# Embeddings stored feature by feature in blocks of 32 samples, Gram products over samples 16 apart

## The chip, the cores and the metric

The kernel runs on one core of one Trainium2 chip. Times are device microseconds of one launch; the kernel's time is the median of its runs.

## The reference, cut to what matters

A recommendation tower for 2,048 samples. Each of 27 tables gives a sample one row of 128 numbers. All pairs of these 27 rows are multiplied (351 dot products a sample), 16 dense inputs are appended, and three layers follow.

```python
e = jnp.stack([tbl_0[ids[:, 0]], ..., tbl_26[ids[:, 26]]], axis=1)   # (2048, 27, 128)
interactions = jnp.einsum('bnd,bmd->bnm', e, e)
z = interactions[:, i, j]                    # i < j, 351 columns
h = jnp.concatenate([z, dense_ctx], axis=1)  # 367 columns
h = jnp.maximum(h @ W_top1 + b_top1, 0.0)    # 512
h = jnp.maximum(h @ W_top2 + b_top2, 0.0)    # 256
y = h @ W_top3                               # 1
```

Eleven tables have 1,000 rows, the other 16 have 1,250 to 125,000. All data are float32.

## The kernel before, in words

The batch is worked in 8 pairs of tiles, 128 samples a tile, 256 a pair. The index p is the pair, t the tile in it.

**Embeddings.** For 16 features GpSimd gathers the rows from HBM by indirect DMA (L543), one sample a partition. TensorE transposes them, four features into one PSUM bank (L583), and ScalarE copies the bank into `emb` (`take_turned`, L871). The 11 small tables lie in SBUF, each split in a rounded part and a rest. VectorE makes one-hot matrices from the ids (L747), TensorE multiplies both parts with them (L572, L574), and ScalarE copies the result into `emb` (`take_lookup`, L852). Most lookups serve two pairs at once; the half for the next pair goes to `held` (L851) and from there to `emb` at the start of the next pair (`place_held`, L862). `emb` holds on each of 128 partitions (one for each of the 128 numbers of a row) tile, sample and feature, the feature innermost, so that the 27 features of a sample are neighbours.

**Gram products.** `gram_products` (L586 to L603) takes four samples a step. Two matmuls, one for each half of the array's output rows, have two samples' 54 columns each as stationary and as moving operand. Their result has the products of each sample with itself on its diagonal blocks, and the products between the two samples beside them, which nobody uses. Eight such steps fill a PSUM bank, four banks make a tile. A plain float32 matmul is two records in the trace, so there are 2,048 records for 1,024 matmuls. ScalarE copies each bank into `gram` (`take_gram`, L882), its columns turned so that the samples of a pair lie innermost.

**The way to layer 1.** The two samples of a half are apart in `gram`'s partitions. SyncE stores the four quarters of `gram` to HBM (`store_products`, L371 to L377, 32 partitions each, for which `stored_rows`, L307, gives the rows) and loads them back as `z` (`load_z`, L415), with every product on a partition of its own. The reload order folds the symmetric matrix. ScalarE puts the dense inputs into `z` (`place_dense`, L904), in the order of the quarters; SyncE had loaded them to one of two buffers (`load_dense`, L360). Layer 1 is L617 on TensorE with L891 on ScalarE, which also sets the samples' order for layer 2, L626; VectorE does the last one (L784, L789). The last pair is worked tile by tile at the end (L644, L655, L897).

**Order of the work.** Every engine has its order written out. Each engine's program goes pair by pair. TensorE in pair p does the lookups of p with transposes between them, layer 1 of p - 1 with the second tile's transposes, Gram products of tile 0, layer 2 of p - 1, Gram products of tile 1. ScalarE follows it bank by bank. Three PSUM banks take transposes and lookups, two take Gram products. In pair 0 the tables also have to be loaded, rounded (L813), shown in PSUM (L824) and split (L768, VectorE). `picks`, an 11 x 11 identity, is the weight with which TensorE spreads the first ids (L671, L677); it has a buffer of its own.

Of the kernel before, what the change touches and what calls it, by code (L numbers as in the profile page):

```python
# [32 lines left out]
F32R = mybir.dt.float32r  # L33
# [95 lines left out]
GROUPS = P // QUARTERS  # L129
GRAM_COLS = ABREAST * NF  # L130
HALF_ROWS = P // HALVES
GRAM_PART = HALF_ROWS + GRAM_COLS
GROUPS_A_BANK = 8
GRAM_BANKS = 2
# [52 lines left out]
def build(nc, dense_t, ids_rows, ids_onehot, gathered_tables, onehot_tables, w1, w2, w3, b1, b2, out):  # L187
    with ExitStack() as ctx:
# [11 lines left out]
        rows = sb("rows", [P, TILES, NG, DIM])  # L200
        emb = sb("emb", [P, TILES, P, NF])
        gram = sb("gram", [P, ABREAST, NF, RUN])
# [13 lines left out]
        b2_row, w3_row = rows23[:, 0, :], rows23[:, 1, :]  # L216
        dense = sb("dense", [P, 2, PAIR])
        held = sb("held", [P, HELD, PAIR])
        h1 = sb("h1", [P, M1, PAIR])

        y = sb("y", [P, 2, TILES])
        last_row = dense[0:1, 0, 0:P]

# [15 lines left out]
        first_ids = table_lo[0:NO, NO - 1, 0:2 * PAIR // DIM, :].rearrange("k j d -> k (j d)")  # L239
        picks = sb("picks", [NO, NO], F32R)  # L240

# [13 lines left out]
        HALF_TABLE = part // GRAM_BANKS  # L255

        idx_loaded = [sem(f"idx_loaded{i}") for i in range(2)]
        ids_first = sem("ids_first")
# [5 lines left out]
        weights_loaded = sem("weights_loaded")  # L264
        dense_loaded = [sem(f"dense_loaded{i}") for i in range(2)]
        dense_placed = sem("dense_placed")
# [40 lines left out]
        def stored_rows(q):  # L307

            half, s = divmod(q, ABREAST)
            row = half * HALF_ROWS + s * NF  # L310

            pad = PAD if q == QUARTERS - 1 else 0
            return row - pad, row - pad + STORE_ROWS, PAD - pad

# [17 lines left out]
        def store_position(engine, t, q):  # L332
            row, end, to = stored_rows(q)
            engine.dma_start(last_products[t, to:to + STORE_ROWS, :, q, :],
                             gram[row:end, q % ABREAST, :, t * GROUPS:(t + 1) * GROUPS]
                             ).then_inc(last_products_out[t], 16)
# [4 lines left out]
        def _(sp):  # L341
# [14 lines left out]
            def load_dense(p):  # L356
                if p >= 2:

                    sp.wait_ge(dense_placed, p - 1)
                sp.dma_start(dense[DENSE_AT:DENSE_AT + DENSE, p % 2, :], dense_t[:, p * PAIR:(p + 1) * PAIR]  # L360
                             ).then_inc(dense_loaded[p % 2], 16)

# [8 lines left out]
            def store_products(p):  # L371

                sp.wait_ge(gram_taken, (p + 1) * PAIR_GRAMS)
                for q in range(QUARTERS):
                    row, end, to = stored_rows(q)
                    sp.dma_start(products[p % 2, to:to + STORE_ROWS, :, q, :], gram[row:end, q % ABREAST, :, :]  # L376
                                 ).then_inc(products_out, 16)  # L377
# [68 lines left out]
            load_dense(0)  # L446
            load_dense(1)
            for i in lookups_of(1)[:IDS_SLOTS]:
                load_ids(i)

            for p in range(PAIRS):
                if p > 0:
                    for i in lookups_of(p)[IDS_SLOTS:]:
                        load_ids(i)
                    store_products(p - 1)
                    load_z(p - 1)
                    if p + 1 < PAIRS:
                        load_dense(p + 1)
                if 0 < p < LAST:
                    for i in lookups_of(p + 1)[:IDS_SLOTS]:  # L460
                        load_ids(i)
                if 0 < p < PAIRS - 1:
                    store_y(p - 1)
# [85 lines left out]
        def _(pe):  # L549
# [36 lines left out]
            def gram_products(p, t):  # L586

                pe.wait_ge(emb_taken, tile_end(p, t))
                for i in range(TILE_GRAMS):
                    a = p * PAIR_GRAMS + t * TILE_GRAMS + i  # L590
                    if a >= GRAM_BANKS:

                        pe.wait_ge(gram_taken, a - GRAM_BANKS + 1)
                    ps = gram_ps[a % GRAM_BANKS]
                    for b in range(GROUPS_A_BANK):
                        group = i * GROUPS_A_BANK + b
                        for half in range(HALVES):
                            first = group * QUARTERS + half * ABREAST
                            samples = emb[:, t, first:first + ABREAST, :].rearrange("d s f -> d (s f)")
                            last = nc.tensor.matmul(  # L600
                                ps[half * HALF_ROWS:half * HALF_ROWS + GRAM_COLS, b * GRAM_COLS:(b + 1) * GRAM_COLS],
                                samples, samples, start=True, stop=True)
                    last.then_inc(gram_full, 1)  # L603
# [17 lines left out]
            def layer2(p):  # L621

                pe.wait_ge(mlp_taken, p * M1 + M1)
                for t in range(TILES):
                    for k in range(M1):
                        last = nc.tensor.matmul(mlp_ps[t][:, 0:HID2], h1[:, k, t * P:(t + 1) * P], w2_sb[:, k, :],  # L626
                                                start=k == 0, stop=k == M1 - 1)
                    last.then_inc(mlp_full, 1)
# [95 lines left out]
        def _(dve):  # L724
            def make_onehot(i, part):
# [19 lines left out]
                if i < NO:  # L745
# [3 lines left out]
                    *operands, ALU.is_equal).then_inc(onehot_ready, 1)  # L749

            dve.wait_ge(ids_first, 16)
            nc.vector.tensor_copy(first_ids, first_ids_i).then_inc(ids_first_f, 1)
# [56 lines left out]
        def _(act):  # L809
# [35 lines left out]
            def take_lookup(i):  # L845
# [4 lines left out]
                if pairs == 2:  # L850
                    nc.scalar.copy(held[:, k if k < len(SETS[0]) else k - len(SETS[0]), :], ps[:, PAIR:2 * PAIR]).then_inc(held_taken, 1)  # L851
                nc.scalar.copy(emb[:, :, :, NG + k], ps[:, 0:PAIR].rearrange("d (t b) -> d t b", t=TILES)  # L852
                               ).then_inc(emb_taken, 1)

            def place_held(p):

                for n, (group, p0, pairs) in enumerate(LOOKUPS):
                    if p0 == p - 1 and pairs == 2:

                        act.wait_ge(held_taken, sum((pairs - 1) * len(SETS[g]) for g, _, pairs in LOOKUPS[:n + 1]))  # L860
                        slot, size = NG + SETS[group][0], len(SETS[group])
                        nc.scalar.copy(emb[:, :, :, slot:slot + size].rearrange("d t b f -> d (t b) f"),  # L862
                                       held[:, 0:size, :].rearrange("d f b -> d b f")).then_inc(held_placed, 1)

                        act.wait_ge(held_placed, sum(pairs - 1 for _, _, pairs in LOOKUPS[:n + 1]))

            def take_turned(p, t, n):
                act.wait_ge(turned, turns_before(p, t, n + 1))
                first, size = turn_bank(n)
                ps = emb_ps[BANK_INDEX[("turn", p * TILES + t, n)] % EMB_BANKS]  # L870
                nc.scalar.copy(emb[:, t, :, first:first + size],  # L871
                               ps[:, 0:size * P].rearrange("d (f b) -> d b f", f=size)).then_inc(emb_taken, 1)

            def take_gram(p, t):
# [3 lines left out]
                for i in range(TILE_GRAMS):  # L878
# [3 lines left out]
                    nc.scalar.copy(  # L882
                        gram[0:GRAM_PART, :, :, g0:g0 + GROUPS_A_BANK].rearrange("r s j g -> r (s j) g"),
                        gram_ps[a % GRAM_BANKS][0:GRAM_PART, 0:GROUPS_A_BANK * GRAM_COLS].rearrange(
                            "r (g c) -> r c g", c=GRAM_COLS)).then_inc(gram_taken, 1)

            def take_layer1(chunk, m):
                act.wait_ge(mlp_full, chunk + m + 1)
                samples = mlp_ps[m % 2][:, 0:PAIR].rearrange("p (r t g) -> p t g r", r=QUARTERS // TILES, t=TILES)
                placed = h1[:, m, :].rearrange("p (t g r) -> p t g r", t=TILES, r=QUARTERS // TILES)  # L890
                nc.scalar.activation(placed, samples, ACT.Relu, bias=b1_sb[:, m:m + 1]).then_inc(mlp_taken, 1)  # L891

            def take_last_layer1(t, m):
                act.wait_ge(mlp_full, LAST * MLP_CHUNKS + t * LAST_CHUNKS + m + 1)
                samples = last1_ps[m][:, 0:P].rearrange("p (q g) -> p g q", q=QUARTERS)
                placed = h1[:, m, t * P:(t + 1) * P].rearrange("p (g q) -> p g q", q=QUARTERS)
                nc.scalar.activation(placed, samples, ACT.Relu, bias=b1_sb[:, m:m + 1]).then_inc(mlp_taken, 1)  # L897

            def place_dense(p):

                act.wait_ge(dense_loaded[p % 2], (p // 2 + 1) * 16)
# [8 lines left out]
            nc.scalar.copy(picks[:, :], ident[0:NO, 0:NO]).then_inc(picks_placed, 1)  # L910
            ahead = EMB_BANKS + 1
# [98 lines left out]
```

## Time and profile before

| | |
|---|---|
| median of 3 runs | 347.89 us (347.8 to 348.27) |
| span of the profiled execution | 346.3 us |
| TensorE matmuls busy | 331.1 us |
| TensorE weight loads busy | 282.8 us |
| VectorE busy | 219.4 us |
| ScalarE busy | 184.7 us |
| GpSimd busy | 242.9 us |
| 16 DMA engines | 44.06 MB moved |

The span is from the first to the last instruction of one profiled execution; the time of a run also holds what lies around it, here 1.6 us to the median. PE is TensorE's matmuls, PEld its weight loads, which run beside them. ACT is ScalarE, DVE VectorE, POOL GpSimd, SP SyncE; a q behind a name is the engine's sequencer, which issues DMAs. Matmuls are pipelined: the mean duration of one is longer than the time between two starts, so the pace of a row of matmuls is read from the time of the whole row.

### The profile page before, as it was taken

Reading aid. Unit: us, or ns where it says so; the run is one execution under the profiler, and the core shown is the slowest. Engines: PE = TensorE matmul, PEld = TensorE weight load, DVE = VectorE, ACT = ScalarE, POOL = GpSimd, SP = SyncE. Lnnn points to the kernel's source line nnn. Section 1 sums busy time; section 2 is a strip of 40 time slices with the busy share of each in tenths; the row PEclk is TensorE's granted clock in tenths of the full one; section 3 lists DMA queues with packets and bytes.
Section 4 is the critical chain, followed back from the end, with each engine's and each line's share of the span. In section 5 each row is a group of like instructions: output and inputs, shape, how many; then the busy total and the mean of one; then the engine's idle time right before and its main releaser. Section 6 shows DMA issues by size and latency. Waiting matters only on the chain.

```text
span 346.3 us, 8212 instructions
## 1 busy us (share of the span) xinstructions
PE 331.1 (96%) x3478; PEld 282.8 (82%) x3478; DVE 219.4 (63%) x160; ACT 184.7 (53%) x315; POOL 242.9 (70%) x263
## 2 busy tenths in 40 slices
PE   2899999999999999999999999999999999998995
PEld 1667878887898888887898889887888889997894
DVE  5899997599427971499626991399724990360021
ACT  4898975533646354633646355633447346554521
POOL 6777777777777777777777777777777777777200
PEclk9999999999999999999999999999999999999999
DMA  6975795655237772768229772677327552572440
GB/s 169 222 178 168 225 252 142 156 157 135 67 55 157 146 158 55 107 173 178 83 55 157 146 160 55 89 197 177 83 57 134 131 112 57 85 168 72 85 81 8
DMA packets 53981, 44.06 MB, mean 127 GB/s; under 512 B 39810, under 2 KB 43983, under 8 KB 53945
## 3 DMA queue, kind: packets, MB, share of 16 engines
q1 hardware_dynamic: 43993, 26.52, 35.1%
q0 software_dynamic: 8192, 16.79, 21.3%
q8 instruction: 28, 0.46, 0.6%
q10 hardware_dynamic: 1760, 0.22, 0.4%
q14 instruction: 8, 0.07, 0.1%
HBM read 36.43 MB, written 7.09 MB: 126 GB/s over the span
## 4 chain that ended last, share of the span: by engine, by line
PE 86%; DMA 6%; SPq 3%; ACT 2%; issue 1%; DVE 1%; DVEq 0%
PE emb_ps L572 21%; PE emb_ps L574 20%; PE gram_ps L600 16%; PE mlp_ps L617 11%; PE mlp_ps L626 7%; PE emb_ps L583 7%; DMA h<-tbl_rows 3%; DMA products<-gram 1%; DMA gram<-tbl_rows 1%; PE emb_ps L644 1%; SPq L376 1%; DMA z<-products 1%; SPq L369 1%; PE mlp_ps L671 1%; PE mlp_ps L655 1%
## 5 line engine op out<-in xcount | busy, mean ns | idle before, releaser
L543 POOL DMA_INDIRECT rows<-tbl_rows,idx x256 | 242.0, 945 | 78.9 <-issue 74.4
L747 DVE TENSOR_TENSOR onehot<-ids_b,row_id 125x2048 fp32r<-125x2048 int32 x72 | 158.9, 2279 | 33.3 <-PE emb_ps L574 33.3
L572 PE MATMUL emb_ps<-onehot,table_hi 125*128 125x512 f32 (+1 forms) x400 | 147.6, 378 | 5.6 <-DVE table_lo L768 4.0
L574 PE MATMUL emb_ps<-onehot,table_lo 125*128 125x512 f32 (+1 forms) x400 | 143.0, 367 | 0.0
L572 PEld LDWEIGHTS emb_ps<-onehot,table_hi 125*128 125x128 f32 x400 | 76.0, 190 | 21.5 <-DVE table_lo L768 4.8
L574 PEld LDWEIGHTS emb_ps<-onehot,table_lo 125*128 125x128 f32 x400 | 76.1, 190 | 10.7
L600 PEld LDWEIGHTS gram_ps<-emb 128*54 128x54 f32 x2048 | 53.6, 130 | 5.6 <-issue 3.5
L600 PE MATMUL gram_ps<-emb 128*54 128x54 f32 x2048 | 55.8, 214 | 1.7 <-ACT emb L852 0.8
L851 ACT COPY held<-emb_ps 128x256 f32<-128x256 f32 x38 | 14.1, 371 | 75.9 <-PE emb_ps L574 75.8
L784 DVE TENSOR_TENSOR mlp_ps<-mlp_ps,rows 128x256 f32<-128x256 f32 x14 | 6.1, 433 | 76.5 <-PE mlp_ps L626 76.5
L882 ACT COPY gram<-gram_ps 118x432 f32<-118x432 f32 x64 | 33.2, 519 | 39.5 <-PE gram_ps L600 39.2
L871 ACT COPY emb<-emb_ps 128x512 f32<-128x512 f32 x64 | 45.5, 710 | 0.0
L617 PE MATMUL mlp_ps<-z,w_sb 126*128 126x256 f32 x168 | 41.2, 380 | 1.0 <-DMA z<-products 1.0
L583 PE MATMUL emb_ps<-ident,rows 128*128 128x128 f32 x256 | 38.8, 274 | 0.0
L852 ACT COPY emb<-emb_ps 128x256 f32<-128x256 f32 x50 | 34.4, 688 | 7.9 <-PE emb_ps L574 7.9
L583 PEld LDWEIGHTS emb_ps<-ident,rows 128*128 128x128 f32 x256 | 31.0, 140 | 7.2 <-issue 0.5
L747 DVE TENSOR_TENSOR onehot<-z,mlp_ps 125x2048 fp32r<-125x2048 int32 (+1 forms) x16 | 33.5, 2114 | 2.0 <-PE mlp_ps L671 1.3
L617 PEld LDWEIGHTS mlp_ps<-z,w_sb 126*128 126x128 f32 x168 | 30.1, 190 | 4.7 <-DMA z<-products 1.2
L626 PE MATMUL mlp_ps<-w_sb,h 128*128 128x256 f32 x112 | 26.0, 386 | 0.0
L626 PEld LDWEIGHTS mlp_ps<-w_sb,h 128*128 128x128 f32 x112 | 20.7, 190 | 2.9
L891 ACT ACTIVATE h<-mlp_ps,columns 128x256 f32<-128x256 f32 x28 | 13.3, 474 | 17.6 <-PE mlp_ps L617 17.6
L862 ACT COPY emb<-held 128x1280 f32<-128x1280 f32 (+1 forms) x7 | 19.2, 2741 | 0.2
(49 smaller groups left out, 102.6 us busy)
## 6 DMA issues: line engine op xcount, KB each, us to landing
ids_b<-ids_onehot SPq DMA_DIRECT2D x33, 256.0 KB, 5.5
products<-gram SPq DMA_DIRECT2D x28, 216.0 KB
gram<-tbl_rows SPq DMA_DIRECT2D x9, 480.0 KB
rows<-tbl_rows,idx POOLq DMA_INDIRECT x256, 2.9
z<-products SPq DMA_DIRECT2D x14, 126.0 KB
h<-tbl_rows SPq DMA_DIRECT2D x2, 480.0 KB
z<-products SPq DMA_DIRECT2D x7, 112.0 KB
w_sb<-w SPq DMA_DIRECT2D x1, 768.0 KB, 5.8
```

The source lines that it names most:

```text
L543: pool.indirect_dma_start(out=rows[:, t, f, :], out_offset=None, in_=gathered_tables[f], in_offset=bass.IndirectOffsetOnAxis(ap=idx[:, p, ...
L572: nc.tensor.matmul(ps[:, 0:width], table_hi[0:ROWS, k, j, :], columns[:, c, :], start=j == 0, stop=False)
L574: last = nc.tensor.matmul(ps[:, 0:width], table_lo[0:ROWS, k, j, :], columns[:, c, :], start=False, stop=j == ROWS_PER - 1)
L583: last = nc.tensor.transpose(ps[:, f * P:(f + 1) * P], rows[:, t, first + f, :], ident[:])
L600: last = nc.tensor.matmul(ps[half * HALF_ROWS:half * HALF_ROWS + GRAM_COLS, b * GRAM_COLS:(b + 1) * GRAM_COLS], samples, samples, start=Tr ...
L617: last = nc.tensor.matmul(ps[:, 0:PAIR], w1_sb[0:k, s, m * P:(m + 1) * P], z[0:k, s, :], start=s == 0, stop=s == STEPS - 1)
L626: last = nc.tensor.matmul(mlp_ps[t][:, 0:HID2], h1[:, k, t * P:(t + 1) * P], w2_sb[:, k, :], start=k == 0, stop=k == M1 - 1)
L747: nc.vector.tensor_tensor(onehot[0:ROWS, seq % ONEHOT_RING, 0:own * width].rearrange("p (j b) -> p j b", b=width), *operands, ALU.is_equal ...
L852: nc.scalar.copy(emb[:, :, :, NG + k], ps[:, 0:PAIR].rearrange("d (t b) -> d t b", t=TILES)).then_inc(emb_taken, 1)
L862: nc.scalar.copy(emb[:, :, :, slot:slot + size].rearrange("d t b f -> d (t b) f"), held[:, 0:size, :].rearrange("d f b -> d b f")).then_in ...
L871: nc.scalar.copy(emb[:, t, :, first:first + size], ps[:, 0:size * P].rearrange("d (f b) -> d b f", f=size)).then_inc(emb_taken, 1)
L882: nc.scalar.copy(gram[0:GRAM_PART, :, :, g0:g0 + GROUPS_A_BANK].rearrange("r s j g -> r (s j) g"), gram_ps[a % GRAM_BANKS][0:GRAM_PART, 0: ...
```

## The change

`emb` becomes `[partition, tile, quadrant of 32 samples, 28 slots, 32 samples]`: the samples of a feature are neighbours, in runs of 32. Slot 28 holds zeros, cleared once by VectorE, and TensorE waits for that once. A Gram product takes two samples 16 apart, so the columns (feature, sample) are 56 elements with one step of 16 elements between them. They come out with the two samples alternating, so a quarter's rows in `gram` are every second partition. One PSUM bank now serves one quadrant. All copies into `emb`, `place_dense` and the layer 1 copies follow the new order, and layer 2 takes every second column of `h1` as weights. To make room, the dense inputs have one buffer (a load waits until the previous pair's were placed), and `picks` lies in an unused corner of the last table.

```diff
-GRAM_COLS = ABREAST * NF
+QUADRANTS = 4
+QUADRANT = P // QUADRANTS
+APART = QUADRANT // ABREAST
+SLOTS = NF + 1
+GRAM_COLS = ABREAST * SLOTS
-GROUPS_A_BANK = 8
+GROUPS_A_BANK = APART // HALVES
...
-        emb = sb("emb", [P, TILES, P, NF])
+        emb = sb("emb", [P, TILES, QUADRANTS, SLOTS, QUADRANT])
-        dense = sb("dense", [P, 2, PAIR])
+        dense = sb("dense", [P, PAIR])
-        picks = sb("picks", [NO, NO], F32R)
+        picks = table_lo[0:NO, NO - 1, 2 * PAIR // DIM, 0:NO]
...
         def stored_rows(q):
-            half, s = divmod(q, ABREAST)
-            row = half * HALF_ROWS + s * NF
-            pad = PAD if q == QUARTERS - 1 else 0
-            return row - pad, row - pad + STORE_ROWS, PAD - pad
+            s, half = divmod(q, HALVES)
+            pad = PAD if half == HALVES - 1 else 0
+            row = half * HALF_ROWS + s - pad * ABREAST
+            return slice(row, row + (STORE_ROWS - 1) * ABREAST + 1, ABREAST), s, PAD - pad
...
             def load_dense(p):
-                if p >= 2:
-                    sp.wait_ge(dense_placed, p - 1)
-                sp.dma_start(dense[DENSE_AT:DENSE_AT + DENSE, p % 2, :], dense_t[:, p * PAIR:(p + 1) * PAIR]
-                             ).then_inc(dense_loaded[p % 2], 16)
+                if p >= 1:
+                    sp.wait_ge(dense_placed, p)
+                sp.dma_start(dense[DENSE_AT:DENSE_AT + DENSE, :], dense_t[:, p * PAIR:(p + 1) * PAIR]
+                             ).then_inc(dense_loaded, 16)
...
             load_dense(0)
-            load_dense(1)
...
                     load_z(p - 1)
-                    if p + 1 < PAIRS:
-                        load_dense(p + 1)
+                    load_dense(p)
...
             def gram_products(p, t):
+                if p == 0 and t == 0:
+                    pe.wait_ge(pads_cleared, 1)
...
-                        group = i * GROUPS_A_BANK + b
                         for half in range(HALVES):
-                            first = group * QUARTERS + half * ABREAST
-                            samples = emb[:, t, first:first + ABREAST, :].rearrange("d s f -> d (s f)")
+                            samples = emb[:, t, i, :, :].rearrange(
+                                "d k (s j) -> d (k s) j", s=ABREAST)[:, :, half * GROUPS_A_BANK + b]
...
-                        last = nc.tensor.matmul(mlp_ps[t][:, 0:HID2], h1[:, k, t * P:(t + 1) * P], w2_sb[:, k, :],
+                        last = nc.tensor.matmul(mlp_ps[t][:, 0:HID2], h1[:, k, t:PAIR:TILES], w2_sb[:, k, :],
...
+            nc.vector.memset(emb[:, :, :, NF, :], 0.0).then_inc(pads_cleared, 1)
             dve.wait_ge(ids_first, 16)
...
-                nc.scalar.copy(emb[:, :, :, NG + k], ps[:, 0:PAIR].rearrange("d (t b) -> d t b", t=TILES)
-                               ).then_inc(emb_taken, 1)
+                nc.scalar.copy(emb[:, :, :, NG + k, :], ps[:, 0:PAIR].rearrange(
+                    "d (t q j) -> d t q j", t=TILES, q=QUADRANTS)).then_inc(emb_taken, 1)
...
-                        nc.scalar.copy(emb[:, :, :, slot:slot + size].rearrange("d t b f -> d (t b) f"),
-                                       held[:, 0:size, :].rearrange("d f b -> d b f")).then_inc(held_placed, 1)
+                        nc.scalar.copy(emb[:, :, :, slot:slot + size, :].rearrange("d t q f j -> d (t q) f j"),
+                                       held[:, 0:size, :].rearrange("d f (q j) -> d q f j", j=QUADRANT)
+                                       ).then_inc(held_placed, 1)
...
-                nc.scalar.copy(emb[:, t, :, first:first + size],
-                               ps[:, 0:size * P].rearrange("d (f b) -> d b f", f=size)).then_inc(emb_taken, 1)
+                nc.scalar.copy(emb[:, t, :, first:first + size, :],
+                               ps[:, 0:size * P].rearrange("d (f q j) -> d q f j", f=size, q=QUADRANTS)
+                               ).then_inc(emb_taken, 1)
...
-                        gram[0:GRAM_PART, :, :, g0:g0 + GROUPS_A_BANK].rearrange("r s j g -> r (s j) g"),
+                        gram[0:GRAM_PART, :, :, g0:g0 + GROUPS_A_BANK],
                         gram_ps[a % GRAM_BANKS][0:GRAM_PART, 0:GROUPS_A_BANK * GRAM_COLS].rearrange(
-                            "r (g c) -> r c g", c=GRAM_COLS)).then_inc(gram_taken, 1)
+                            "r (g c s) -> r s c g", s=ABREAST, c=SLOTS)[:, :, 0:NF, :]).then_inc(gram_taken, 1)
...
-                samples = mlp_ps[m % 2][:, 0:PAIR].rearrange("p (r t g) -> p t g r", r=QUARTERS // TILES, t=TILES)
-                placed = h1[:, m, :].rearrange("p (t g r) -> p t g r", t=TILES, r=QUARTERS // TILES)
+                samples = mlp_ps[m % 2][:, 0:PAIR].rearrange("p (q x g) -> p x q g", q=QUARTERS, g=GROUPS_A_BANK)
+                placed = h1[:, m, :].rearrange("p (x q g) -> p x q g", q=QUARTERS, g=GROUPS_A_BANK)
...
-                        z[DENSE_PART:DENSE_PART + DENSE, STEPS - 1, c0:c1].rearrange("d (q g) -> d q g", q=QUARTERS),
-                        dense[DENSE_AT:DENSE_AT + DENSE, p % 2, c0:c1].rearrange("d (g q) -> d q g", q=QUARTERS))
+                        z[DENSE_PART:DENSE_PART + DENSE, STEPS - 1, c0:c1].rearrange(
+                            "d (q x g) -> d q x g", q=QUARTERS, g=GROUPS_A_BANK),
+                        dense[DENSE_AT:DENSE_AT + DENSE, c0:c1].rearrange(
+                            "d (x q g) -> d q x g", q=QUARTERS, g=GROUPS_A_BANK))
```

## Rows read from the trace of the kernel before

**Rows 1.** The page: busy time and share of each engine; granted clock in slices.
```profile
PE 331.1 (96%) x3478; PEld 282.8 (82%) x3478; DVE 219.4 (63%) x160; ACT 184.7 (53%) x315; POOL 242.9 (70%) x263
...
PEclk9999999999999999999999999999999999999999
```

**Rows 2.** The page: the chain that ended last, by engine and line.
```profile
PE emb_ps L572 21%; PE emb_ps L574 20%; PE gram_ps L600 16%; PE mlp_ps L617 11%; PE mlp_ps L626 7%; PE emb_ps L583 7%; DMA h<-tbl_rows 3%; DMA products<-gram 1%; DMA gram<-tbl_rows 1%; PE emb_ps L644 1%; SPq L376 1%; DMA z<-products 1%; SPq L369 1%; PE mlp_ps L671 1%; PE mlp_ps L655 1%
```

**Rows 3.** Waits on TensorE's queues: who waited <- for whom: us, times, longest.
```profile
PE mlp_ps L617 <- DMA z<-products: 1.0, 1, 1.0
PE gram_ps L600 <- ACT emb L852: 0.8, 1, 0.8
PE gram_ps L600 <- ACT emb L871: 0.7, 1, 0.7
PE emb_ps L572 <- ACT emb L852: 0.7, 2, 0.4
...
PEld emb_ps L572 <- ACT emb L852: 2.0, 4, 0.6
```

**Rows 4.** ScalarE's groups by form: xcount | busy us, mean ns | idle before.
```profile
L871 ACT COPY emb<-emb_ps 128x512 f32<-128x512 f32 x64 | 45.5, 710 | 0.0
L852 ACT COPY emb<-emb_ps 128x256 f32<-128x256 f32 x50 | 34.4, 688 | 7.9 <-PE emb_ps L574 7.9
L882 ACT COPY gram<-gram_ps 118x432 f32<-118x432 f32 x64 | 33.2, 519 | 39.5 <-PE gram_ps L600 39.2 <-issue 0.3
L851 ACT COPY held<-emb_ps 128x256 f32<-128x256 f32 x38 | 14.1, 371 | 75.9 <-PE emb_ps L574 75.8
L862 ACT COPY emb<-held 128x1280 f32<-128x1280 f32 x4 | 10.1, 2532 | 0.1
L862 ACT COPY emb<-held 128x1536 f32<-128x1536 f32 x3 | 9.1, 3019 | 0.1
L904 ACT COPY z<-dense 16x256 f32<-16x256 f32 x7 | 4.5, 646 | 0.2
L904 ACT COPY z<-dense 16x128 f32<-16x128 f32 x2 | 0.7, 418 | 1.4 <-issue 1.4
L930 ACT COPY rows<-mlp_ps 128x512 f32<-128x512 f32 x1 | 0.6, 586 | 0.2 <-PE mlp_ps L664 0.2
```

**Rows 5.** The chain in order of time, first pair: start us, us, what.
```profile
44.36 0.55 ACT emb L852
...
54.00 0.67 ACT emb L852
```

**Rows 6.** Busy time in a stretch (PE, PEld, DVE, ACT, POOL); VectorE's last-but-one split.
```profile
40.00:50.00 10.00, 8.95 (x64) 7.54 (x63) 10.00 (x10) 8.55 (x15) 7.56 (x9) 1.00 1.05 287
...
47.06 1.27 DVE L768 TENSOR_TENSOR table_lo<-gram,gram_ps 125x512 fp32r<-125x512 f32 x2
```

**Rows 7.** The chain in order of time, around the last pair.
```profile
304.08 4.54 DMA products<-gram
...
324.98 0.66 ACT emb L871
```

**Rows 8.** The chain in order of time: a lookup, transposes, layer 1, a Gram tile.
```profile
26.82 0.23 PE emb_ps L574
...
91.19 0.44 PE emb_ps L583 x4
91.62 1.30 PE mlp_ps L617 x6
...
93.36 3.42 PE gram_ps L600 x128
```

**Rows 9.** The weight loads of L600: duration ns min/median/max, first and last start.
```profile
L600 PEld LDWEIGHTS gram_ps<-emb x2048: 124/130/130, 54.7 to 328.9; 128*54 128x54 f32 x187
```

**Rows 10.** SyncE in order of time, pair 1: the issue of the dense load.
```profile
72.35 0.53 SPq L360 DMA_DIRECT2D dense<-dense_t  x1
```

**Rows 11.** All engines at the start, in order of time.
```profile
2.88 0.41 DVE L752 CAST table_lo<-rows 11x512 fp32r<-11x512 int32 x1 [2.88 <-DMA rows<-ids_onehot]
```

More of the change, by code:

```diff
@@ L221, in build @@
         y = sb("y", [P, 2, TILES])
-        last_row = dense[0:1, 0, 0:P]
+        last_row = dense[0:1, 0:P]
         row_id_i = z[:, STEPS - 1, 0:ROWS_PER].bitcast(I32)
@@ L255, in build @@
         HALF_TABLE = part // GRAM_BANKS
+        pads_cleared = sem("pads_cleared")
         idx_loaded = [sem(f"idx_loaded{i}") for i in range(2)]
@@ L264, in build @@
         weights_loaded = sem("weights_loaded")
-        dense_loaded = [sem(f"dense_loaded{i}") for i in range(2)]
+        dense_loaded = sem("dense_loaded")
         dense_placed = sem("dense_placed")
@@ L332, in store_position @@
         def store_position(engine, t, q):
-            row, end, to = stored_rows(q)
+            rows_of, s, to = stored_rows(q)
             engine.dma_start(last_products[t, to:to + STORE_ROWS, :, q, :],
-                             gram[row:end, q % ABREAST, :, t * GROUPS:(t + 1) * GROUPS]
+                             gram[rows_of, s, :, t * GROUPS:(t + 1) * GROUPS]
                              ).then_inc(last_products_out[t], 16)
@@ L374, in store_products @@
                 for q in range(QUARTERS):
-                    row, end, to = stored_rows(q)
-                    sp.dma_start(products[p % 2, to:to + STORE_ROWS, :, q, :], gram[row:end, q % ABREAST, :, :]
+                    rows_of, s, to = stored_rows(q)
+                    sp.dma_start(products[p % 2, to:to + STORE_ROWS, :, q, :], gram[rows_of, s, :, :]
                                  ).then_inc(products_out, 16)
@@ L894, in take_last_layer1 @@
                 act.wait_ge(mlp_full, LAST * MLP_CHUNKS + t * LAST_CHUNKS + m + 1)
-                samples = last1_ps[m][:, 0:P].rearrange("p (q g) -> p g q", q=QUARTERS)
-                placed = h1[:, m, t * P:(t + 1) * P].rearrange("p (g q) -> p g q", q=QUARTERS)
+                samples = last1_ps[m][:, 0:P].rearrange("p (q x g) -> p x q g", q=QUARTERS, g=GROUPS_A_BANK)
+                placed = h1[:, m, t * P:(t + 1) * P].rearrange("p (x q g) -> p x q g", q=QUARTERS, g=GROUPS_A_BANK)
                 nc.scalar.activation(placed, samples, ACT.Relu, bias=b1_sb[:, m:m + 1]).then_inc(mlp_taken, 1)
             def place_dense(p):
-                act.wait_ge(dense_loaded[p % 2], (p // 2 + 1) * 16)
+                act.wait_ge(dense_loaded, (p + 1) * 16)
                 spans = [(0, PAIR)] if p < LAST else [(t * P, (t + 1) * P) for t in range(TILES)]
@@ L904, in place_dense @@
                     last = nc.scalar.copy(
-                        z[DENSE_PART:DENSE_PART + DENSE, STEPS - 1, c0:c1].rearrange("d (q g) -> d q g", q=QUARTERS),
-                        dense[DENSE_AT:DENSE_AT + DENSE, p % 2, c0:c1].rearrange("d (g q) -> d q g", q=QUARTERS))
+                        z[DENSE_PART:DENSE_PART + DENSE, STEPS - 1, c0:c1].rearrange(
+                            "d (q x g) -> d q x g", q=QUARTERS, g=GROUPS_A_BANK),
+                        dense[DENSE_AT:DENSE_AT + DENSE, c0:c1].rearrange(
+                            "d (x q g) -> d q x g", q=QUARTERS, g=GROUPS_A_BANK))
                 last.then_inc(dense_placed, 1)
             act.wait_ge(ident_steps, 3)
-            nc.scalar.copy(picks[:, :], ident[0:NO, 0:NO]).then_inc(picks_placed, 1)
+            nc.scalar.copy(picks, ident[0:NO, 0:NO]).then_inc(picks_placed, 1)
             ahead = EMB_BANKS + 1
```

## The prediction
> **What bounds the kernel now.** I read the page's busy line first [rows 1]: TensorE is busy 331.1 of 346.3 us, ScalarE 184.7, VectorE 219.4. Then the chain that ended last [rows 2]: TensorE carries 86% of it, and the Gram products (L600) are 16%, 55 us. Last the waits of TensorE's own queues [rows 3], which tell what a faster ScalarE could give back: TensorE's matmuls waited for ScalarE's embedding copies (L852, L871) 0.8 + 0.7 + 0.7 us, and its weight loads up to 2.0 us in one row, at mostly the same moments. So the kernel is bound by TensorE; ScalarE is a side road. The change makes ScalarE's work lighter and touches what TensorE reads. These two ends decide it. The clock plays no part: the page has it granted in full all through [rows 1].
>
> The sum is made against the profiled span, 346.3 us. The median of the runs, 347.89, lies 1.6 us above it; I carry that over unchanged. A measurement of this kernel can tell a change of about 0.2%, 0.7 us, from none.
>
> **ScalarE's copies.** Two rows give its price for data that lie in a row: 371 ns for 256 elements (L851) and 586 for 512 (L930), so 0.84 ns an element and 156 ns to begin [rows 4]. The copies whose elements jump pay more: L852 (256 elements, each 27 from the next) 688 ns, L862 2532 ns for 1280 and 3019 for 1536, L871 (runs of four) 710 ns for 512. After the change all of them write and read runs of 32 or more. By the two prices they take 371, 1231, 1446 and 586 ns. That frees 50 x 0.317 + 4 x 1.30 + 3 x 1.57 + 64 x 0.124 = 33.7 us of ScalarE. L882 keeps 432 elements and runs of eight; at 519 ns it already stands at the price of a row (156 + 432 x 0.84 = 519), so its jumps in PSUM cost nothing and it stays.
>
> Nearly all of that lies beside TensorE's work. What lies on the path:
> - At 54.00 the last lookup of the first pair is copied (0.67 us) while TensorE stands before its first Gram product [rows 5]. The copy gets 0.3 us shorter: **-0.3 us**.
> - At 44.36 a copy of L852 holds up a lookup by 0.4 us [rows 3, 5]. But VectorE is busy 10.00 of the 10.00 us from 40 to 50 [rows 6], and the lookup after the next one needs its table split, which ends only at 48.33. TensorE would only come early to that: 0, at most -0.3 us.
> - At 324.98 the last turned bank (L871, 0.66 us) holds the last Gram tile [rows 7]: **-0.1 us**.
> These are all the long ones in the list [rows 3]; past the first pair, the last is the only one. Sum of the copies: **-0.4 us**, between -1.0 (0.3 more at 44.36 and 0.3 more at the last tile) and 0.
>
> **The Gram products, number of columns.** 54 columns become 56, in the stationary and the moving operand. A tile's 128 records (64 pairs, one record of a pair for each half of the array) take 3.42 us, 53.4 ns a pair [rows 8]. The wide matmuls give the pace of plain float32: 0.44 us for four of 128 columns, 1.30 for six of 256, so 107 ns for 128 more columns, 0.84 ns each. At that pace 54 columns stream in 45 ns and 56 in 47: both are shorter than the 53.4 ns between pairs, so something fixed may set the interval. If the columns set it, two more cost 2 x 0.84 = 1.7 ns, times 1,024 pairs (2,048 records [rows 9]) 1.7 us. Bounds 0 and +1.7; I take **0**, since the stream is 6 ns shorter than the interval even with 56.
> The Trainium skill (TensorE: Matmul & The Clock Gate, Back-to-back issue gap) has matmuls of 1 to 64 columns all cost about 60 cycles. By that this term is 0 too, against +1.7 by columns; the 26.7 ns a record here speaks for the page.
>
> **The Gram products, where they read.** The two samples' features lay as 54 neighbours. Now each column is 16 elements, 64 bytes, from the last, for both operands. No TensorE row here reads so, so I bound it. From below 0: a plain float32 column takes 0.84 ns, while the lookups read theirs at 0.23 us for 512, 0.45 ns each [rows 8], so the read path can do twice what a Gram record asks, and a reader that fell to half of that would still keep up. From above: ScalarE's copy of the dense inputs (L904) reads SBUF with a step of four elements, 646 ns for 256 and 418 for 128, so 1.78 ns an element against 0.84 [rows 4]. TensorE at 1.78 would need 100 ns for 56 columns, some 105 a pair, and lose 52 x 1,024 = 53 us. The two ends are far apart. I take **0**: the nearest row is one of TensorE itself, and it shows the reserve; but that row reads neighbours, and here two halves and two loads read at once, so the doubt is large and is the main rival.
>
> **Layer 2** takes its weights (L626) with a step of two. A load runs beside the matmul before it; were its stream of 128 columns (107 ns at 0.84 each) doubled, 214 would still fit the 217 of a matmul of 256 [rows 8]. 0, at most 112 records x 15 ns = 1.7 us.
>
> **Stores and loads.** The four stores of a pair keep their bytes and runs; their rows are now every second partition. Only the last pair shows TensorE waiting for their result, 1.0 us [rows 3], behind a flight of the stores of 4.54 us [rows 7]. It stands there once, so everywhere else z lands ahead. I take 0, between -1.0 (that wait gone) and +2 (each store of the last pair half a microsecond slower).
> **Dense inputs in one buffer.** One 16 KB load leaves the start; the others move one pair later. Its new wait on SyncE is for the placement of the pair before. ScalarE makes that between the two Gram tiles of its pair, and SyncE comes to the load only after it has stored both tiles and issued the z loads, at 72.35 in pair 1 [rows 10]: no wait. Queued behind it are the id loads of the next pair and the store of y, as before. The data are due when that pair's first Gram tile is copied, which ends in pair 1 at 93.36 + 3.42 [rows 8], 24 us later; in the last pair they are placed after both Gram tiles. 0. Without that cover it would be one small load's landing, a few microseconds a pair.
> **Picks and pads.** Picks move into a corner of the last table, whose rewriting comes after their last use; no wait is added. Clearing the pads is one VectorE memset of 256 elements; its cast of 512 elements takes 0.41 us [rows 11], so less than that, within VectorE's 2.88 us of idleness at the start [rows 11], and TensorE asks for it at 54.7. 0; without that cover 0.4 us at most. The layer 1 copies and L904 get runs of eight; none is on the path.
>
> Sum: -0.4 + 0 + 0 = -0.4 us: **347.5 us**. This case's own range is 346.9 to 348.4.
>
> **Rivals.**
> 1. *TensorE pays for the jumps* (slower). Place: L600. It decides as soon as one column at a step of 64 bytes takes longer than 0.95 ns (53.4 over 56). For it: every SBUF access of ScalarE with a jump of 16 bytes or more costs it twice, L904, L852 and L862 alike. Against it: the reserve above. At 1.78 ns, 347.5 + 53 = 400.5 us; at just twice the stream, 94 + 3 ns a pair, 347.5 + 44 = 391.5. I put 396, the middle. Chance 0.35. Some 0.07 more for a shared reading port, where both halves queue for it: 190 ns a pair, +140 us, 488.
> The Trainium skill speaks for this rival: SBUF — State Buffer (Door 1: The DMA port swizzle) has lines of 16 bytes, and each access that crosses to a new line pays a penalty. It gives no size. ScalarE's rows agree; no row of TensorE here shows it.
> 2. *Columns set the interval.* 347.5 + 1.7 = 349.2. Chance 0.08.
> 3. *The lighter ScalarE gives back more* (faster): all waits on it go, and the last pair's z comes earlier: -1.0 and -0.6, 346.3. For it: the list of waits. Against: VectorE without a gap from 40 to 50 us. Chance 0.13.
> The change does what it says; only its worth is open.
>
> **How the numbers follow.** Forecast 0.37, rival 1 0.35 and 0.07, rival 2 0.08, rival 3 0.13. The range leaves out the shared port and a little of each side: 346.3 to 403. Faster by over 0.2% (under 347.2): rival 3 and 0.04 of the forecast, 0.17. Within: 0.32. Slower: rivals 1 and 2 and a trace of the forecast, 0.51. Signs are split, so the time is that of the likeliest single case.
>
> **What would show it.** Right: a Gram tile of 128 records still near 3.42 us; L852 near 371 ns, L871 near 586, L862 near 1231 and 1446; ScalarE busy near 151 us; the wait at the first Gram product shorter by 0.3. Wrong: a Gram tile of 6 us or more and a weight load of L600 well over 130 ns [rows 9] (rival 1); 3.53 us (rival 2); a longer z wait in the last pair.

## The result and the profile after

The changed kernel takes 393.38 us (median of 4 runs, 392.94 to 394.59) against 347.93 for the one before in the same job: a ratio of 1.1299, 95% interval 1.1275 to 1.1324. It is 45.5 us slower. The forecast was 347.5; the first rival, that TensorE pays for the jumps, had 391.5 to 400.5.

The page of the changed kernel, busy line and chain, against [rows 1, 2]:

```profile
PE 377.6 (96%) x3478; PEld 330.2 (84%) x3478; DVE 219.9 (56%) x161; ACT 155.3 (40%) x315; POOL 243.1 (62%) x263
...
PEclk9999999999999999999999999999999999999999
...
PE gram_ps L604 26%; PE emb_ps L575 20%; PE emb_ps L577 19%; PE mlp_ps L621 9%; PE emb_ps L586 7%; PE mlp_ps L630 7%; DMA h<-tbl_rows 3%; DMA products<-gram 1%; DMA z<-products 1%; PE emb_ps L648 1%; PE mlp_ps L675 1%; SPq L374 1%; SPq L381 1%; PE mlp_ps L659 0%; PE gram_ps L659 0%
```

ScalarE is busy 29.4 us less, VectorE and GpSimd the same, TensorE 46.5 us more, and its clock is granted as before. The Gram products (now L604) grew from 16% of the chain to 26%. The groups by form, against [rows 4, 9] (xcount | busy us, mean ns | idle before):

```profile
L604 PE MATMUL gram_ps<-emb 128*56 128x56 f32 x2048 | 102.7, 274 | 1.2 <-ACT emb L877 0.7 <-ACT emb L857 0.6
L604 PEld LDWEIGHTS gram_ps<-emb 128*56 128x56 f32 x2048 | 100.3, 190 | 4.8 <-issue 3.8 <-ACT emb L877 0.9
...
L877 ACT COPY emb<-emb_ps 128x512 f32<-128x512 f32 x64 | 38.0, 594 | 0.3
L889 ACT COPY gram<-gram_ps 120x432 f32<-120x432 f32 x64 | 33.2, 520 | 88.4 <-PE gram_ps L604 82.8 <-issue 5.6
...
L857 ACT COPY emb<-emb_ps 128x256 f32<-128x256 f32 x50 | 18.9, 378 | 10.7 <-PE emb_ps L577 10.7
...
L867 ACT COPY emb<-held 128x1280 f32<-128x1280 f32 x4 | 5.1, 1263 | 0.1
L867 ACT COPY emb<-held 128x1536 f32<-128x1536 f32 x3 | 4.4, 1477 | 0.1
```

ScalarE's copies fell nearly as read from its own rows: 378, 594, 1263 and 1477 ns where 371, 586, 1231 and 1446 were expected; L889, the old L882, stayed at 520. A weight load of a Gram product rose from 130 to 190 ns. The chain in order of time, against [rows 5, 7, 8] (start us, us, what):

```profile
54.72 12.62 PE gram_ps L604 x256
67.34 0.43 PE emb_ps L575
...
98.47 6.36 PE gram_ps L604 x109
...
233.00 6.37 PE gram_ps L604 x128
239.37 3.66 PE mlp_ps L630 x16
...
343.30 4.84 DMA products<-gram
...
368.12 0.56 ACT emb L877
```

The same places in the kernel before: its first two Gram tiles, which the next lookup ends, the second tile of a pair, and a row of layer 2. Behind them is the wait for z in the last pair, of the changed kernel ([rows 3] has it for the one before).

```profile
54.72 6.51 PE gram_ps L600 x234
...
62.22 0.43 PE emb_ps L572
...
96.78 3.65 PE mlp_ps L626 x16
100.43 3.37 PE gram_ps L600 x128
```
```profile
PE mlp_ps L621 <- DMA z<-products: 0.4, 1, 0.4
```

A Gram tile takes 6.36 or 6.37 us (the last of the last two pairs 6.39 and 6.44). Before, the first tile of a pair took 3.42 and the second 3.37. (A row of the trace can lack some records, x109 for instance; its time is that of the whole tile.) The first two tiles took 12.62 us; before they ended 7.50 us after their start (54.72 to 62.22), so 5.1 more now. The other 14 rows of the chain add up to 89.2 us against 47.65, 41.55 more. That makes 46.7 us. The wait for the last pair's z gave 0.6 back (1.0 to 0.4; why is not shown), the last turned bank 0.1, and the stretch from the last copy to the end of the trace was 0.5 shorter (2.3 against 2.8). What is left is 45.5, the difference of the spans (391.8 against 346.3). The other matmuls keep their pace, layer 2 with its weights at a step of two among them (3.66 against 3.65 us for 16 records). SyncE and TensorE show no wait for the dense buffer, the picks or the pads.

### The profile page after: what moved, and what is told of

Its sections match the earlier page's. It is cut to its first block, busy times and chain, and to the rows that moved or that the text cites. A ratio compares the mean times of both kernels' runs of the same rounds, so it can differ in the third digit from the quotient of the medians.

```text
span 391.8 us, 8214 instructions
## 1 busy us (share of the span) xinstructions
PE 377.6 (96%) x3478; PEld 330.2 (84%) x3478; DVE 219.9 (56%) x161; ACT 155.3 (40%) x315; POOL 243.1 (62%) x263
## 4 chain that ended last, share of the span: by engine, by line
PE 91%; DMA 5%; SPq 2%; issue 1%; ACT 1%; DVE 0%; DVEq 0%
PE gram_ps L604 26%; PE emb_ps L575 20%; PE emb_ps L577 19%; PE mlp_ps L621 9%; PE emb_ps L586 7%; PE mlp_ps L630 7%; DMA h<-tbl_rows 3%; DMA products<-gram 1%; DMA z<-products 1%; PE emb_ps L648 1%; PE mlp_ps L675 1%; SPq L374 1%; SPq L381 1%; PE mlp_ps L659 0%; PE gram_ps L659 0%
## 5 line engine op out<-in xcount | busy, mean ns | idle before, releaser
L604 PEld LDWEIGHTS gram_ps<-emb 128*56 128x56 f32 x2048 | 100.3, 190 | 4.8 <-issue 3.8
L604 PE MATMUL gram_ps<-emb 128*56 128x56 f32 x2048 | 102.7, 274 | 1.2 <-ACT emb L877 0.7
L889 ACT COPY gram<-gram_ps 120x432 f32<-120x432 f32 x64 | 33.2, 520 | 88.4 <-PE gram_ps L604 82.8
L877 ACT COPY emb<-emb_ps 128x512 f32<-128x512 f32 x64 | 38.0, 594 | 0.3
L857 ACT COPY emb<-emb_ps 128x256 f32<-128x256 f32 x50 | 18.9, 378 | 10.7 <-PE emb_ps L577 10.7
L829 ACT COPY gram_ps<-table_hi 125x512 f32<-125x512 f32 x22 | 12.3, 596 | 0.6 <-DVE table_lo L773 0.4
```

The source lines that it names most:

```text
L604: last = nc.tensor.matmul(ps[half * HALF_ROWS:half * HALF_ROWS + GRAM_COLS, b * GRAM_COLS:(b + 1) * GRAM_COLS], samples, samples, start=Tr ...
L857: nc.scalar.copy(emb[:, :, :, NG + k, :], ps[:, 0:PAIR].rearrange("d (t q j) -> d t q j", t=TILES, q=QUADRANTS)).then_inc(emb_taken, 1)
L877: nc.scalar.copy(emb[:, t, :, first:first + size, :], ps[:, 0:size * P].rearrange("d (f q j) -> d q f j", f=size, q=QUADRANTS)).then_inc(e ...
L889: nc.scalar.copy(gram[0:GRAM_PART, :, :, g0:g0 + GROUPS_A_BANK], gram_ps[a % GRAM_BANKS][0:GRAM_PART, 0:GROUPS_A_BANK * GRAM_COLS].rearran ...
```

## The experiments

Each is a single run with its profile unless a ratio is given. A time "against" another is against the kernel before in the same job. Where the text says wrong features or columns, the kernel multiplies other data than it should; the number of instructions is the same. "Tile" is a Gram tile's row in the chain, 128 records, or 64 pairs of records (one record of a pair for each half of the array). "Near" stands for 56 neighbouring columns, "line" for 16 bytes of SBUF that begin at a multiple of 16.

**e1: the change without its step.**
```diff
-                            samples = emb[:, t, i, :, :].rearrange(
-                                "d k (s j) -> d (k s) j", s=ABREAST)[:, :, half * GROUPS_A_BANK + b]
+                            flat = emb[:, t, i, :, :].rearrange("d k j -> d (k j)")
+                            c0 = (b * HALVES + half) * GRAM_COLS
+                            near = flat[:, c0:c0 + GRAM_COLS]
...
-                                samples, samples, start=True, stop=True)
+                                near, near, start=True, stop=True)
```


> The changed kernel, but both operands of a Gram product are 56 neighbours of the block (so it multiplies the wrong features); layout, copies, stores, 56 columns, dense buffer and picks are those of the change. Theory (only the 64-byte step costs): a Gram tile of 128 records takes 3.42 us, or 3.53 if columns set the interval; time 347.5 us, or 349.2. Rival (the stores of every second partition, the copies or the wider products carry part of the 45 us): well over 350 us, up to 393 if the step is innocent.

349.6 us against 348.6; ratio 1.0036, interval 1.0024 to 1.0048. Its row in the chain:
```profile
290.26 3.51 PE gram_ps L605 x128
```
All but 1 us is gone with the step. Layout, stores of every second partition, the single dense buffer and the picks are innocent of the 45 us. The tile is 3.51, not 3.42, although nothing but two columns was added to it.

**e9: the same with 54 columns** (`SLOTS = NF`, no clearing of pads).

> As e1 (neighbours for both operands, wrong features), with 27 slots and so 54 columns, and no clearing of pads: all of the change but the step and the two more columns. If two more columns cost 1.67 ns a pair: 50.0 ns a pair, tile 3.42 us, and 1.6 us less than e1, 0.1% under before or equal to it. If 28 slots cost nothing: the same as e1, 0.36% over before.

348.23 us against 348.55; ratio 0.9992, interval 0.9971 to 1.0012; its tile:
```profile
252.04 3.42 PE gram_ps L603 x128
```
Two columns more thus cost 0.09 us a tile, 1.4 us in 16 tiles: the columns do set the interval. What is left of the change, lighter copies included, cannot be told from no change.

**e2 and e3: one operand with the step.** As e1, but `samples, near` (weights apart) or `near, samples` (moving apart).

> Only the stationary operand has the 64-byte step, the moving one is 56 neighbours (wrong features). Theory A (each operand's reader pays by itself, and either sets the interval): Gram tile about 6.36 us, weight load about 190 ns, time 393. Theory B (the two share one budget of reads): tile about 4.9 us, time 370. Theory C (only the moving operand pays): tile 3.4 to 3.5, weight load 130 ns, time 348.

> Only the moving operand has the 64-byte step, the stationary one is 56 neighbours (wrong features). Theory A (each reader pays by itself): tile about 6.36 us, weight load back near 130 ns, time 393. Theory B (shared budget): 4.9 us, 370. Theory D (only weight loads pay): tile 3.4 to 3.5 us, time 348.

394.84 and 393.95 us, tiles of 6.42 and 6.38 us. Weight loads and matmuls of the two kernels, e2 first:
```profile
L607 PE MATMUL gram_ps<-emb 128*56 128x56 f32 x2048 | 103.6, 262 | 1.2 <-ACT emb L880 0.7 <-ACT emb L860 0.6
L607 PEld LDWEIGHTS gram_ps<-emb 128*56 128x56 f32 x2048 | 101.7, 191 | 4.8 <-issue 3.8 <-ACT emb L880 0.9
```
```profile
L607 PE MATMUL gram_ps<-emb 128*56 128x56 f32 x2048 | 102.9, 274 | 1.2 <-ACT emb L880 0.7 <-ACT emb L860 0.6
L607 PEld LDWEIGHTS gram_ps<-emb 128*56 128x56 f32 x2048 | 99.6, 146 | 4.8 <-issue 3.8 <-ACT emb L880 0.9
```
Either operand alone is enough for the whole price, and both together cost no more than one. So theory A holds, the one in which each operand pays by itself and the slower sets the interval. One detail of it missed: with neighbours again in e3, a weight load took 146 ns and not 130. The two runs also say what a repair needs: both operands must be free of the step.

**e4, e10, e5: other blocks, the right result.** The samples of a product are half a block apart, so blocks of 4 give a step of 8 bytes and blocks of 8 one of 16. e4 has 54 columns, e10 and e5 have 56.
```diff
-QUADRANTS = 4
+QUADRANTS = P // 4
...
-GROUPS_A_BANK = APART // HALVES
+GROUPS_A_BANK = 8
+GROUPS_A_BLOCK = APART // HALVES
```
(e5 has `P // 8` and, like e10, keeps the 28th slot; the Gram products pick block and place from b, and the layer 1 copies use `GROUPS_A_BLOCK`.)

> The same layout with blocks of 4 samples instead of 32 and 27 slots: the two samples of a product are 2 apart, so its 54 columns have a step of 2 elements, 8 bytes, and two of them share 16 bytes. The result is the reference's. Theory (what costs is a new 16-byte line for every column; two columns a line are enough for plain float32): tile 3.42 us, L852's copies about as fast as L871's before (runs of four), time 347.3 to 347.7, equal to before. Rival (any step costs): tile up to 6.4 us, 391.

> Blocks of 4 as in e4, but with the 28th slot, 56 columns at a step of 2. The result is the reference's. If the uneven 49 to 54 ns a pair of e4 (51.6 on average with 54 columns) come of blocks of 27 slots that end off a multiple of 32 bytes, the pairs are even here at 51.7 ns. Otherwise they are uneven again, about 53 ns, tile 3.6.

> Blocks of 8 samples, 56 columns with a step of 4 elements, 16 bytes: every column begins a new 16 bytes, though only a quarter of the change's step. The result is the reference's. Line theory (what counts is how many different 16-byte lines the columns touch, 1.67 ns a line): 96.7 ns a pair, tile 6.4 us, 393. Rival (the cost grows with the length of the step): tile between 3.5 and 5 us, 350 to 370.

e4: 349.65 us against 348.6; ratio 1.0037, interval 1.0012 to 1.0062. e10: 351.15 against 348.55. e5: 402.82 against 348.66. One row of the chain of each, in this order:
```profile
299.21 3.50 PE gram_ps L605 x124
```
```profile
320.74 3.59 PE gram_ps L607 x128
```
```profile
365.71 6.94 PE gram_ps L607 x128
```
At 8 bytes the price is 0.1 us a tile (e4 against e9, e10 against e1); at 16 bytes it is all there. It does not grow with the length of the step: 16 bytes cost even more than 64 (6.94 against 6.37), and no run shows why. In e10 the starts of the pairs stay uneven with the 28th slot (53 ns a pair, tile 3.59), so the alignment of the blocks is not what makes them uneven.

**e6: a step of 12 bytes.**
```diff
+                            c0 = b * 88 + half * 8
+                            samples = flat[:, c0:c0 + 3 * GRAM_COLS - 2:3]
```


> The changed kernel, but both operands read 56 columns with a step of 3 elements, 12 bytes (wrong features). Four columns touch three lines. Line theory: 56 x 0.75 x 1.67 = 70 ns and 3 to 5 more, 74 ns a pair, tile 4.9 us, time 369. Threshold theory (a step under 16 bytes is free, from 16 on it costs twice): 51.7 ns, tile 3.5, 349. Threshold at 8 bytes: 96.7 ns, tile 6.4, 393.

376.83 us against 348.66:
```profile
352.90 5.25 PE gram_ps L605 x128
```
The tiles take 5.16 to 5.29 us (one took 6.17). That is neither of the thresholds' values (3.5 and 6.4) and 5 to 8% over the 4.9 by lines at 1.67 ns. The price for a line is not one number: at that of e5 (6.94 us for 56 lines) the 42 lines here come to 5.2. So the price goes with the number of lines that the columns touch, with an open end of 9% between the steps of 16 and 64 bytes.

**e7: twos of neighbours, a long jump after each** (moving operand `emb[:, t, i, :, j0:j0 + 2]`, weights neighbours).

> The changed kernel with its block layout, but the moving operand takes two neighbouring samples of each feature (28 times 2 elements, 128 bytes from one two to the next), the stationary one 56 neighbours (so the products are of wrong features). Two columns a line with a long jump after each two. Line theory: 28 lines x 1.67 = 47 ns, at the pace of the array: 51.7 ns a pair, tile 3.5, time 349. Rival (a long jump itself costs): over 60 ns a pair, 360 or more.

351.35 us:
```profile
321.03 3.65 PE gram_ps L607 x120
```
3.65 us for the first tile of a pair and 3.68 for the second, 0.14 and 0.22 over neighbours (3.51 and 3.46 in e1). A jump of 128 bytes is nearly free as long as two columns share a line. (The weights were not tried so.)

**e12: a layout with neighbours for TensorE, the right result.** Based on the kernel before; blocks of two samples (`BLOCKS` is 64, `BLOCK` is 2), so the 54 columns (feature, sample) are adjacent.
```diff
-        emb = sb("emb", [P, TILES, P, NF])
+        emb = sb("emb", [P, TILES, BLOCKS, NF, BLOCK])
...
-                            samples = emb[:, t, first:first + ABREAST, :].rearrange("d s f -> d (s f)")
+                            samples = emb[:, t, block, :, :].rearrange("d f s -> d (f s)")
```


> The kernel before with another layout that leaves TensorE its neighbours: blocks of 2 samples, feature by feature, so the 54 columns of a product (feature, sample) are adjacent, and ScalarE writes runs of two. Dense buffers, picks and layer 2 as before. The result is the reference's. Tile 3.42 us, 50 ns a pair. If ScalarE pays by lines, L852 falls from 688 to about 371 ns (two elements a line); time 347.9 - 0.4, so equal to before or 0.1% faster. Rival (the stores of every second partition cost): over 348.6 on the scale of 347.9.

348.59 us against 348.66; ratio 1.0003, interval 0.9986 to 1.002. Its rows:
```profile
L872 ACT COPY emb<-emb_ps 128x512 f32<-128x512 f32 x64 | 38.7, 605 | 0.6 <-PE emb_ps L584 0.5
...
L852 ACT COPY emb<-emb_ps 128x256 f32<-128x256 f32 x50 | 20.5, 410 | 10.4 <-PE emb_ps L575 10.4
```
```profile
251.87 3.42 PE gram_ps L600 x128
```
Runs of two give ScalarE nearly all of its gain (410 ns where runs of 32 have 378 and single elements had 688) and TensorE loses nothing. It is what the change wanted, and it buys nothing: ScalarE is not the bound.

**Why TensorE had no reserve: e13 to e16.** Two theories were left. One: every stream of columns needs 1.67 ns for a line, whatever else is read. The other: the two halves of the array share a port that gives a line in 0.83 ns.

e13: as e3, but only the first half's moving operand has the step (`moving = samples if half == 0 else near`).

> Stationary operands are neighbours; of the moving ones only that of the first half has the 64-byte step, the second half's is neighbours (wrong features). Shared-port theory (one 16-byte line in 0.83 ns for both halves' moving data together): 56 + 14 = 70 lines a pair, 58 ns, so 58 to 65 ns a pair, tile 3.9 to 4.3 us, about 358. Per-stream theory (each stream needs 1.67 ns for a line): the slow half sets the pair, 97 ns, tile 6.4, 393.

e14: the kernel before, layer 2 with a step in its moving operand.
```diff
-                        last = nc.tensor.matmul(mlp_ps[t][:, 0:HID2], h1[:, k, t * P:(t + 1) * P], w2_sb[:, k, :],
+                        last = nc.tensor.matmul(mlp_ps[t][:, 0:HID2], h1[:, k, t * P:(t + 1) * P],
+                                                w2_sb[:, :, :].rearrange("p k n -> p (k n)")[:, k:M1 * HID2:M1],
```


> The kernel before, but layer 2, a plain float32 matmul over the whole array, reads its 256 moving columns with a step of 4 elements, 16 bytes (wrong weights). Shared-port theory: a single stream at 0.83 ns a column needs one line in 0.83 ns and gets it: 216 ns a record as now, time 348. Per-stream theory: 427 ns a record, 112 records, +24 us, 372.

e15 and e16: the output rows are `ps[0:GRAM_COLS, ...]` for both halves, with the step (e15) and with neighbours (e16).

> The changed kernel with its step of 64 bytes, but both halves' products go to the same 56 output rows, one after the other, so that only one moving stream runs at a time (half of the products are lost). Shared-port theory: 47 ns of stream and 3 to 5 a record, 100 to 103 ns a pair, tile 6.4 to 6.7 us, the same as with neighbours in the next run. Per-stream theory: 97 ns a record, 193 a pair, tile 12.4, about 490 us.

> As the run before, with neighbours for both operands (wrong features). Both theories: 100 to 103 ns a pair, tile 6.4 to 6.7 us, about 394. It is the base for that run: what differs is the price of the step for one stream alone.

e13 took 394.31 us, e14 375.08, e15 493.73, e16 399.95, beside 349.0 for the kernel before. Chain rows of e13, e14, e15 and e16, one fence each:
```profile
199.81 6.38 PE gram_ps L608 x69
```
```profile
349.18 3.44 PE gram_ps L600 x128
352.62 7.42 PE mlp_ps L626 x16
```
```profile
462.22 12.68 PE gram_ps L604 x128
```
```profile
374.75 6.82 PE gram_ps L605 x128
```
e13, e14 and e15 against e16 speak for the price of each stream by itself. In e13 one slow half set the pair: 6.38 us a tile, where the shared port would have given 3.9 to 4.3. In e14 layer 2 has the whole array to itself, and its 16 records went from 3.65 to 7.42 us. With one place for both halves a Gram record takes 53 ns with neighbours (6.82 us / 128, e16) and 99 with the step (12.68 / 128, e15). e16 itself, the base, came out 1.5% above what was expected of it (399.95 us, 394 expected). The shared port is refuted.

**e8 and e17: the float32r lookups with a step.** float32r is the rounded form of float32 in which the one-hot matrices and the split tables are stored (`fp32r` in the rows). These runs are the kernel before, with the one-hot columns, the moving operand, read with a step of 2 or 4 elements, or as twos 32 bytes apart. The cut is of the run with step 2.
```diff
+                    flat = onehot[0:ROWS, (piece + part) % ONEHOT_RING, :]
+                    starts = [min(c * width, ROWS_PER * PAIR - 2 * width) for c in range(chunks)]
+                    columns = [flat[:, c0:c0 + 2 * width:2] for c0 in starts]
```


> The kernel before, but the lookups (float32r, a column in 0.42 ns) read their moving operand with a step of 2 elements, 8 bytes (wrong ids' columns). Line theory in nanoseconds (1.67 ns a line, whatever the format): 0.83 ns a column, a matmul of 512 columns 427 ns and more against 228 now, so 608 wide and 192 narrow ones add 608 x 0.21 + 192 x 0.10 = 149 us, some 497 us. Rival (two columns a line are enough at any pace): no change, 348.

> The same with a step of 4 elements, 16 bytes. Line theory: 1.67 ns a column, 853 ns for 512, adding 608 x 0.64 + 192 x 0.32 = 450 us, some 800 us. Rival (a new line costs one more cycle at the pace of the format, so just double the column): 427 ns for 512, some 500 us.

> The kernel before, but the lookups (float32r) read their moving operand as twos of neighbours, 32 bytes from one two to the next (wrong ids' columns). Theory of eight bytes at a time (float32r reaches 0.42 ns a column only by taking two neighbours in one reading, and a new line at each reading costs it nothing): no change, 348 us. Line theory (1.67 ns for every new 16-byte line also here, which would leave step 4 unexplained): 0.83 ns a column, 451 ns for 512, 497 us.

497.57, 504.63 and 503.82 us, against 348.55, 348.55 and 347.66. The wide lookups of step 2, of step 4 and of the twos, whose group had 123.3 us busy before:
```profile
L574 PE MATMUL emb_ps<-onehot,table_hi 125*128 125x512 f32 x304 | 195.8, 644 | 4.0 <-DVE table_lo L770 4.0
```
```profile
L574 PE MATMUL emb_ps<-onehot,table_hi 125*128 125x512 f32 x304 | 200.9, 661 | 4.0 <-DVE table_lo L770 4.0
```
```profile
L573 PE MATMUL emb_ps<-onehot,table_hi 125*128 125x512 f32 x304 | 200.3, 659 | 4.0 <-DVE table_lo L769 4.0
```
The price comes one step earlier than in plain float32, at 8 bytes, and does not double again at 16. The rule in nanoseconds a line foresaw the first (497) and missed the second (800 expected, where its rival, double the column, said 500); the rule of eight bytes at a time missed e17. What float32r does inside is open. Shown is that all three patterns with gaps lose its pace, for the moving operand; its weights were not tried.

## Why the prediction was wrong

- **What bounds the kernel**: right. A load taken off ScalarE (29.4 us busy) gave nothing that can be measured (e9, e12), a load put on TensorE counted in full.
- **ScalarE's copies, -0.4 us**: prices right within 8 ns for two of the forms and 32 for the others. Busy time fell by 29.4 us and not by 33.7, since the records of neighbouring copies overlap, before more than after; the durations of all ScalarE records together fell by 35.4. The gain on the path did not come whole. The first pair's last copy did shrink from 0.67 to 0.38 us, but the first Gram product starts at 54.72 in both traces, as that copy starts 0.2 us later (54.00 and 54.21). Both chains there go back to the landing of table rows, at 14.25 us before and 14.52 after; in e12 and e4 it was at 14.81 and 15.41, so a single trace cannot show a gain of 0.3.
- **Two more columns, 0**: wrong. I took the time of a whole tile over 64 as the interval, 53.4 ns. That held the beginning and the end of the row; from start to start the pairs repeat every 50 ns in the trace of the kernel before, 52 in that of e1. The 6 ns by which the stream was said to be shorter than the interval were no gap that two columns could use. e1 against e9 measured 1.4 us, the bound named was 1.7.
- **The step of 64 bytes, 0**: wrong, and this is the step of the sum that failed. The text argued that the lookups read a column in 0.45 ns, so that "a reader that fell to half of that would still keep up". That reserve was read off another format, float32r, and off neighbours, four columns a line; float32r loses its own pace with gaps (e8, e17). With a line for each column a plain float32 stream has none (e14, e15 against e16). Measured: 2.86 us a tile over e1, 45.3 us over the 16 tiles of the two traces, 45 ns a pair for 56 columns, so 0.8 ns a column on top of 0.84.
- **Rival 1** was right in place, kind and size: twice the stream gave 391.5, 393.4 was measured. Its chance was 0.35 against 0.37 for the forecast, so the choice between them was close. The row that should have weighed more was L904 [rows 4]: ScalarE's reads at a step of 16 bytes paid 1.78 ns instead of 0.84, and TensorE's plain float32 stream has the same 0.84 ns a column to lose. (That L904, L852 and L862 all pay "twice" is loose: by [rows 4] L852 pays 2.08 ns an element, 2.5 times.) The page of the Trainium skill named there (SBUF — State Buffer, Door 1: The DMA port swizzle) was on this side too; it also says that two hits on a line are needed for the full rate, and e4, e6 and e7 agree with that for plain float32 (+0.1, +1.7 and +0.14 to +0.22 us a tile). For float32r two columns a line were not enough (e8, e17), and there the measurement decides.
- **Shared port** (0.07): refuted by e13 and e14.
- **The rule of the Trainium skill** (TensorE: Matmul & The Clock Gate, Back-to-back issue gap), that 1 to 64 columns cost the same, does not hold for this case: the two more columns did cost, 3.51 against 3.42 us a tile.
- **Layer 2 at a step of two, stores, dense buffer, picks, pads, each 0**: right. e1 holds all of them and is 1.0 us over before, and the columns alone are 1.4.

## What to carry to other kernels

Lay the data out for the engine that bounds the kernel. Count for both operands of a matmul how many different 16-byte lines their columns touch. In plain float32 let at least two columns share a line; in float32r leave the moving columns neighbours. Do not read a reserve off a row of another format or pattern. If the engine that bounds the kernel is the one that now reads the jumps, price them at twice the stream until measured. A layout halfway (blocks of two, e12) can serve both engines.

## What was not expected of the hardware

- One slow operand costs as much as two: 6.4 us a tile for weights apart (e2), moving apart (e3) or both.
- A step of 16 bytes cost more than one of 64: tile 6.94 (e5) against 6.37 us.
- Two array halves side by side are worth 3.3 us a tile (3.51 in e1 against 6.8 in e16).
- ScalarE's writes: runs of four that fill a line cost no more than runs of 32 (378 and 594 ns in e4). The old runs of four features, every 27 elements and so beginning anywhere in a line, cost 710 instead of 594; that the place in the line is the reason is not shown, as the order of the reads from PSUM differs too.
